# A fused cross-attention and sparse feed-forward kernel: norm factors through HBM instead of a second transposition

## What is computed

```python
q = layernorm(x)                       # over the 512 columns, b = 32, c = 64, n = 512
qh, kh, vh = Wq q, Wk ctx, Wv ctx      # 8 heads of 64
qh = softmax(qh, over the 64 of a head) * 64 ** -0.5
kh = softmax(kh, over n)
context = einsum('bhdn,bhen->bhde', kh, vh)
out = Wo @ einsum('bhde,bhdn->bhen', context, qh) + bo        # b, 64, 512
norm = maximum(sqrt(sum(out * out, over the 64 channels)), 1e-12)
x = x + out / norm * g * 8             # g: one gain per channel

y = layernorm(x)                       # feed-forward on 2048 rows of 512
inter = y @ c1.T @ c2.T                # rank 16, 1792 wide
idx = argmax of each block of 32 in inter                      # 56 per row
out = relu(w1[idx] @ y) @ w2t[idx]
return x + out
```

## Time and profile before

| | before |
|---|---|
| median of 3 runs | 764.79 us |
| the profiled execution | 764.77 us, span 762.7 us |
| granted TensorE clock | 0.991 of full (2.4 GHz) |
| TensorE busy | 739.2 us, 97% |
| DVE busy | 624.0 us, 82% |
| GpSimd busy | 486.9 us, 64% |
| ACT busy | 402.3 us, 53% |
| DMA | 66,376 packets, 55.23 MB, 40,704 of them under 512 B |

### The profile page before, as it was taken

The page is one execution under the profiler, slowest core; times in us unless marked ns, Lnnn a source line. Parts: engine busy times, 40 slices in busy tenths (PEclk is TensorE's granted clock), DMA queues, the critical chain, the costliest instruction groups (busy, mean ns, idle before and its releaser), DMA issues.

```text
span 762.7 us, 14646 instructions
## 1 busy us (share of the span) xinstructions
PE 739.2 (97%) x5210; PEld 565.2 (74%) x5210; DVE 624.0 (82%) x910; ACT 402.3 (53%) x773; POOL 486.9 (64%) x549
## 2 busy tenths in 40 slices
PE   8989999999999999999995999999999999999998
PEld 6555665665665666665664989989898998989896
DVE  7978999999999999999956778787777878777652
ACT  5879999999999999998831112102111110211010
POOL 3899999998888888677554363463536346363420
PEclk9999999999999999999997999999999999999999
DMA  6244334333333333221201203022130311211011
GB/s 166 63 113 118 104 102 130 97 105 104 98 81 97 94 83 97 70 72 56 76 18 26 78 20 105 21 52 76 24 102 21 104 21 49 78 22 49 20 53 34
DMA packets 66376, 55.23 MB, mean 72 GB/s; under 512 B 40704, under 2 KB 49536, under 8 KB 66304
## 3 DMA queue, kind: packets, MB, share of 16 engines
q1 hardware_dynamic: 65648, 53.57, 25.8%
q10 hardware_dynamic: 656, 0.72, 0.3%
HBM read 38.52 MB, written 8.39 MB: 62 GB/s over the span
## 4 chain that ended last, share of the span: by engine, by line
PE 71%; POOL 17%; DVE 4%; issue 3%; ACT 2%; SPq 2%; DMA 1%; DVEq 0%; POOLq 0%; ACTq 0%
PE slot L1113 20%; PE po L1131 10%; PE turn L1131 10%; PE po L1243 7%; POOL Q L534 7%; PE turn L1228 5%; PE slot L1269 4%; PE turn L1211 4%; PE slot L1283 3%; POOL weights_lo L483 3%; POOL c_low L516 2%; POOL x_low L473 2%; SPq L275 2%; PE slot L1095 2%; PE po L1254 1%
## 5 line engine op out<-in xcount | busy, mean ns | idle before, releaser
L534 POOL TENSOR_TENSOR Q<-Q,qrec 128x1024 f32<-128x1024 f32 x64 | 121.4, 1905 | 36.3 <-DVE qrec L775 36.3
L422 POOL TENSOR_TENSOR E<-E,rank 128x512 bf16<-128x512 bf16 (+1 forms) x64 | 71.1, 1111 | 108.6 <-DVE E L624 107.6
L1246 PE MATMUL po<-QT,G 128*64 128x512 f32 x256 | 116.9, 599 | 0.0
L1243 PE MATMUL po<-E,ctxT 128*64 128x512 f32 x256 | 116.9, 599 | 0.0
L945 ACT ACTIVATE E<-slot,neg_kmax 128x512 f32<-128x512 f32 x128 | 86.3, 686 | 8.8 <-DVE neg_kmax L761 8.5
L435 POOL TENSOR_TENSOR behind<-E,first 128x512 bf16<-128x512 bf16 (+1 forms) x64 | 60.4, 944 | 41.9 <-DVE first L632 41.7
L727 DVE TENSOR_REDUCE qmax<-slot 128x16 f32<-128x1024 f32 x64 | 75.3, 1217 | 12.6 <-PE slot L1283 12.6
L1243 PEld LDWEIGHTS po<-E,ctxT 128*64 128x64 f32 x256 | 32.3, 136 | 65.4 <-issue 58.5
L761 DVE TENSOR_REDUCE neg_kmax<-slot 128x2 f32<-128x1024 f32 x64 | 76.4, 1194 | 3.8 <-PE slot L1269 2.9
L767 DVE TENSOR_REDUCE qsum<-Q 128x16 f32<-128x1024 f32 x64 | 77.3, 1208 | 2.2 <-ACT Q L934 1.5
L953 ACT ACTIVATE E<-turn 128x512 f32<-128x512 f32 x128 | 74.8, 612 | 3.7 <-PE turn L1211 2.7
(11 more groups left out here) (185 smaller groups left out, 1970.0 us busy)
## 6 DMA issues: line engine op xcount, KB each, us to landing
c_in<-in_ctx SPq DMA_DIRECT2D x64, 128.0 KB, 2.6
x_in<-in_x SPq DMA_DIRECT2D x64, 128.0 KB, 2.6
stage<-in_ffn_w SPq DMA_DIRECT2D x32, 225.0 KB, 2.6
attn_out<-po_sb SPq DMA_DIRECT2D x32, 128.0 KB, 2.3
out<-E SPq DMA_DIRECT2D x16, 256.0 KB, 2.3
ctxT<-in_ctxT SPq DMA_DIRECT2D x31, 128.0 KB, 2.5
attn<-attn_out SPq DMA_DIRECT2D x9, 256.0 KB, 3.6
E<-attn_out SPq DMA_DIRECT2D x7, 256.0 KB, 4.0
```

Of the source, the lines that this page charges most:

```text
L534: nc.gpsimd.tensor_tensor(half, half, qrec[1 - par][:, s, :].unsqueeze(2).broadcast_to([P, HALF, D]), ALU.mult).then_inc(q_scaled, 1)
L1243: nc.tensor.matmul(po[0:C, :], ctxT[1 - par][:, m, :], E[1 - par][:, :, m * P:(m + 1) * P], start=(m == 0), stop=(m == NT - 1)).then_inc(p ...
L1246: nc.tensor.matmul(po[C:P, :], G[:, m, :], QT[m][:], start=(m == 0), stop=(m == HT - 1)).then_inc(out_mm, 1)
```

## The change

The transposed attention output is used for the norm alone. The squares stay in PSUM. The inverse norms, `[128 partitions, 8]` per tile (column n = 128 t + p, for batch b), are stored number by number into a new HBM buffer `factors` of shape `[16, 2, 512]`, and loaded back as a tile of `[128, 512]` in which the 512 numbers of a batch are repeated on its 64 channel partitions. DVE (for tiles 0 and 1 GpSimd) multiplies the attention output, which was never turned, by that tile. `turn_back`, `keep_turned` and `scale_kept` are gone.

```diff
-FIRST_ITEMS, PAIRS = 2, 12
+FIRST_ITEMS, PAIRS = 4, 14
+TURNS = (B - 8, B - 5)
+        over_channels = lambda a: factors[a].unsqueeze(1).broadcast_to([2, C, N])
+        by_token = lambda f: f.rearrange("b (t p) -> p (b t)", p=P)
+        inverted = lambda a: a + 1 if a < 2 else 2 + a // 2
...  SP, attention steps
+                def store_factor(a):
+                    sp.wait_ge(norm_inv, a + 1)
+                    sp.dma_start(by_token(factors[a]), inv[:, a], allow_slow_non_contiguous=True).then_inc(first_stored, 16)
+                def load_factor(a):
+                    sp.wait_ge(first_stored, 16 * (a + 1))
+                    sp.dma_start(spread_of(a), over_channels(a)).then_inc(spread_in[a], 16)
-                    if real(known, -2):
+                    if real(known, -2) and known < B + 1:
                         sp.wait_ge(po_copied, g)
                         sp.dma_start(scratch[g - 2], po_sb[par][C:P, :]).then_inc(stored[par], 16)
...  SP, duo
-                            sp.wait_ge(attn_turned, a - 1)
+                            sp.wait_ge(added, a - 1)
                             load_attn(a)
...  GpSimd
+                def scale(a):
+                    pool.wait_ge(spread_in[a], 16)
+                    nc.gpsimd.tensor_tensor(attn_of(a), attn_of(a), spread_of(a), ALU.mult).then_inc(scaled, 1)
                 def duo(d, last):
-                    rank_mask(d, 3)
-                    select(d, 2)
-                    rank_mask(d, 4)
                     select(d, 3)
                     if not last:
-                        invert(2 * d + 2)
+                        invert(2 * d + 2, 2)
                     rank_mask(d, 5)
                     select(d, 4)
-                    if not last:
-                        invert(2 * d + 3)
                     select(d, 5)
...  DVE
                 def scale(a):
-                    dve.wait_ge(norm_inv, a + 1)
-                    dve.wait_ge(attn_back, max(a - 1, 2))
-                    nc.vector.tensor_tensor(by_batch(turned_of(a)), by_batch(pre[t][:]), ...)
+                    dve.wait_ge(spread_in[a % 2], 16 * (a // 2 + 1))
+                    nc.vector.tensor_tensor(attn_of(a), attn_of(a), spread_of(a), ALU.mult).then_inc(scaled, 1)
                 def duo(d, last):
...
                     gate(d, 1)
-                    if not last:
-                        scale(a + 1)
                     block_max(d, 6)
                     h_low(d, 1)
-                    if not last:
-                        residual(a, pre[0])
                     gate(d, 2)
+                    if not last:
+                        for t in range(2):
+                            scale(a + t)
+                            residual(a + t)
+                            moments_of(a + t)
+                        normalize(a)
                     first_max(d, 6)
+                        normalize(a + 1)
                     block_max(d, 7)
...  ACT
+                def exchange(d):
+                    a = 2 * d + 2
+                    act.wait_ge(norm_inv, inverted(a))
+                    for t in range(2):
+                        nc.scalar.dma_start(by_token(factors[a + t]), inv[:, t], allow_slow_non_contiguous=True)\
+                            .then_inc(factors_stored, 16)
+                    act.wait_ge(factors_stored, 32 * (d + 1))
+                    act.wait_ge(scaled, a)
+                    for t in range(2):
+                        nc.scalar.dma_start(spread_of(a + t), over_channels(a + t)).then_inc(spread_in[t], 16)
                 def duo(d, last):
                     h_high(d, 0)
                     if not last:
-                        square(a, pre[0])
-                        square(a + 1, pre[1])
+                        exchange(d)
                     h_high(d, 1)
...  ACT, step
+                        if known == B + 1:
+                            act.wait_ge(po_copied, g)
+                            nc.scalar.dma_start(scratch[g - 2], po_sb[par][C:P, :]).then_inc(stored[par], 16)
...  TensorE, duo
-                    if not last_duo:
-                        turn_attn(a, pre[0])
-                        turn_attn(a + 1, pre[1])
...
-                        turn_back(a, pre[0])
-                        turn_back(a + 1, pre[1])
...
                     down(d, 3)
+                    if d + 2 < DUOS:
+                        turn_attn(a + 2, pre[0])
+                        turn_attn(a + 3, pre[1])
```

More of the change, by code:

```diff
@@ L78, in real, with program @@
     return known is None or 0 <= known + shift < B
-def program(nc, A, scratch, out):
+def program(nc, A, scratch, factors, out):
     with ExitStack() as ctx:
@@ L542, in step @@
                         bias(g + 2, par)
[L543 to L551, removed]
+                    if known in TURNS:
+                        invert(TURNS.index(known), 1)
+                    if known in (TURNS[0] + 1, TURNS[1] + 1):
+                        scale(TURNS.index(known - 1))
+                    if known in (B - 4, B - 2):
+                        prepare((known - (B - 4)) // 2)
+                        normalize((known - (B - 4)) // 2)
                     if known == B - 1:
@@ L671, in duo @@
                     gate(d, 1)
-                    if not last:
-                        scale(a + 1)
                     block_max(d, 6)
                     h_low(d, 1)
+                    gate(d, 2)
                     if not last:
-                        residual(a, pre[0])
-                    gate(d, 2)
+                        for t in range(2):
[3 more added lines that the diff above has]
+                        normalize(a)
                     first_max(d, 6)
                     if not last:
-                        residual(a + 1, pre[1])
-                    h_low(d, 2)
+                        normalize(a + 1)
                     block_max(d, 7)
[L684 to L687, removed]
                     if not last:
@@ L690, in duo @@
                         xT_rest(a + 1, pre[1])
+                    h_low(d, 2)
+                    first_max(d, 7)
                     gate(d, 3)
-                    h_low(d, 3)
                     gate(d, 4)
@@ L695, in duo @@
                         z_low(d + 1)
-                    h_low(d, 4)
+                    h_low(d, 3)
                     if not last:
@@ L1056, in turn_attn @@
                     last.then_inc(attn_turned, 1)
-                def turn_back(a, bank):
-                    pe.wait_ge(scaled, a + 1)
-                    if a < 2:
-                        pe.wait_ge(q_copied, HT * (B - 5 + a) + 4)
-                    for t in range(NT):
-                        last = nc.tensor.transpose(bank[:, t * P:(t + 1) * P], turned_of(a)[:, t * P:(t + 1) * P], ident[:])
-                    last.then_inc(attn_back, 1)
                 def turn_x(a, bank):
@@ L1145, in duo @@
                         down(d - 1, 6)
-                    else:
-                        project(d, 5)
                     project(d, 6)
                     hide(d, 2)
-                    if not last_duo:
-                        turn_back(a, pre[0])
-                        turn_back(a + 1, pre[1])
                     down(d, 0)
@@ L1292, in step @@
                         pe.wait_ge(rest_in, 32)
-                    if known in (B - 3, B - 2):
-                        turn_back(known - (B - 3), turn[(8 * g + 1) % 3])
+                    if known in TURNS:
+                        turn_attn(TURNS.index(known), turn[(8 * g) % 3])
+                    if known in (B - 2, B - 1):
+                        turn_x(known - (B - 2), turn[(8 * g) % 3])
                     for m in range(HT):
@@ L1314, in step @@
                     turn_e(3)
[L1315 to L1318 removed]
                     if known == B:
[L1320 removed]
                         project(0, 2)
                         project(0, 3)
+                        hide(0, 0)
+                        project(0, 4)
                     if known == B + 1:
[L1324 removed]
+                        turn_attn(2, pre[0])
+                        turn_attn(3, pre[1])
+                        project(0, 5)
                 steps(step)
```

191 lines of the change are left out of this document (94 added, 97 removed).

## The result

The changed kernel takes 911.5 us (median of four runs, 910.8 to 912.7) against 766.75 for the kernel before on the same chip: ratio 1.189 [1.184, 1.193], +145 us. The forecast was 822 us with a range of 747 to 850. The direction was right; the time is outside the range. The profiled execution took 910.75 us and has a span of 909.1.

A forecast was written before the change was run, and what follows sets the result against it. TensorE was taken as the bound, with 71% of the chain of waits and no slack in the duos. The terms 38 + 10 + 4.6 + 7.5 - 3 = +57 gave 822 us, its own range 780 to 860, all cases 747 to 850.

The forecast's parts named there:

- The chain's reading: Last 340 us, eight duos of 44.67 us: TensorE never waits, so any wait added ahead of a matmul is lost.
- The load: Repeating factor loads in a duo: confined to two DMA engines, landing 8.2 and 13.7 us after issue.
- Rival A: Whole kernel: repeating load confined by its outermost count of 2; duo 51 us, 822 us in all; chance 0.52.
- Rival B: Whole kernel: load spread over 16 engines, 4-byte writes at most 37 ns; 752 us (744 to 760); chance 0.33.
- Items: Attention loop: weight items start at step 4, two at a time for 14 steps; -3 us (-2 to -3.5).
- The wait of 3.4 us in step 3: Attention loop, step 3: TensorE's 3.42 us wait for GpSimd goes when its two pairs of items leave.
- The stores: Duo's 4-byte stores to HBM: 30 ns a packet, 3.8 us, plus 2.3 for a plain store and 0.5 issue.
- It adds nothing of its own: Duo: stores sharing engines with mask transposes, and SP's second half of masks behind load_attn, add no time of their own.
- ACT's blocked h_high(d,1): Duo: h_high stands behind ACT's wait for the stores; costed at nothing, with TensorE waiting at down(d,1) as its sign.
- the seam's delay of 4.6: Seam before the duos: with two engines the second load is in at 426.3, turn_x ends at 431.6, +4.6 us.
- 38 + 10 + 4.6: Us added: 38 over six duos, 10 for the slowed clock in seven duos, 4.6 at the seam.
- The attention end: End of attention loop: GpSimd's scale(0) and scale(1) wait for the round trip; -0.5, or +7.5 us (0 to +12).

The follow-up runs named there:

- the run with 32-byte rows: Changed kernel with inverse norms stored as 128 rows of 32 bytes instead of 1,024 single numbers per tile, loads unchanged, norms applied to wrong tokens: 816.2 us, ratio 1.067.
- both edits together: Changed kernel with inverse norms stored in 32-byte rows and repeating loads split to outermost count 64, norms applied to wrong tokens: 753.7 us, ratio 0.984.
- The run with stores alone: Changed kernel with its 4-byte stores, but only two rows of each factor tile loaded in the duos: 832.7 us, ratio 1.088.

## Why the prediction was wrong, step by step

**Right.** The chain's reading: a duo had no slack, and idle before turn_x went into the time. The load: two engines, 8.2 and 13.7 us forecast, 8.6 and 13.8 measured with cheap stores. By the Trainium skill ("DMA: Bandwidth & Descriptors", "Why a DMA increments its semaphore by 16 and not by 1") the outermost counts set the number of engines; here the load with an outermost count of 2 ran at a DMA share of 0.13, two of sixteen, and took 10.4 to 15.8 us, and with 64 it took 3.4 to 4.3, so the trace agrees. Rival A's duo of 51 us is the 51.3 of the run with 32-byte rows, and its 822 us that run's 816. Rival B's 752 is the 753.7 of both edits together. Items: -3 forecast, -3.1 measured. The wait of 3.4 us in step 3 is gone.

**The step that failed: "The stores".** I had each land 6.1 us after issue (2.3 + 3.8); in the duos it was 11.8. I took 30 ns per 4-byte piece on an engine, with 60 as the end. Between 128 and 16 pieces an engine (if spread over sixteen) the landing differs by 11.8 - 2.0 = 9.8 us, 88 ns a piece. Nor is the form of the term right, a price times the number of pieces: from 2.0 us for 16 pieces an engine, 88 ns would give a lone store of 1,024, 64 an engine, 6.2 us, and it took 11.4 and 9.9. The bound came from queue 1's mean packet, that is from the time that packets occupy in the records. That measure misses the cost: the 12,544 packets more than in the run with 32-byte rows add 2.3% x 16 x 909.1 - 1.8% x 16 x 812.0 = 101 us, 8 ns each, while in the duo above the landing comes 8 us after the last packet. An upper end from packets of 2 KB and 256 bytes was no bound for a write of 4.

**"It adds nothing of its own".** I named the mask transpositions that share engines with the stores and dismissed them. They are most of what the small writes cost in a duo. A transposition issued beside the stores lands with them; DVE is ready for gate(1) at 557.8 (564.99 - 7.21), in time for down(d,1), which TensorE reaches at 563.1 (567.65 - 4.51); it comes 7.2 us later and TensorE idles 4.5. The run with stores alone puts 8.3 us on a duo (51.8 for 43.5) with no wait at turn_x; the loads alone put 7.8 (51.3). Together they make 19.8 instead of 16.1. Most of the difference is at turn_x: per duo TensorE waits 6.6 us at down and 8.9 at turn_x (46.3 and 62.4 over seven), where the stores alone gave 7.0 at down and the loads alone 5.3 at turn_x. Late stores send the loads out late (564.73 - 553.14 = 11.6 us after the store, for 2.4 with 32-byte rows), and the stall at down, 6.6 us, covers only part of that. The forecast had a stall at down as a sign of ACT's blocked h_high(d,1). The stall came, and it was the mask.

**Sum.** From the two kernels' spans, 909.1 - 762.7 = 146.4: 15.5 up to duo 0's inverse (423.3 against 407.8), 113.3 in six duos (379.8 against 266.5), 17.6 behind. The last holds duo 6 with its own round trip. In the forecast the seam's delay of 4.6 is duo 0's turn_x, behind that inverse. So forecast were 53 behind it (38 + 10 + 4.6), measured 131, and 4.5 ahead of it (7.5 - 3), measured 15.5. The attention end went wrong by the same step: the lone stores of 1,024 pieces took 11.4 and 9.9 us where I had 4.2. With 32-byte rows and the same loads the inverse of duo 0 comes at 408.4, 15 us earlier. Rival A's 822 us therefore fits the run with 32-byte rows only because that run takes the stores' cost away: the division of the load was right, and the stores were not.

**Small errors.** The inverse ends 4.5 us after the duo's first down matmul (534.78 - 530.32 with both edits), not 2.3; the pow of sixteen takes 3.35 us, not 2.9. ACT's block, costed at nothing, shows no cost in the runs.

What stays open is why a transposition on SP's queue waits for the whole of ACT's small writes and is not served between them, and what makes 4-byte pieces land late when their packets are long over.

## What to carry to other kernels

Look at the size of a DMA's pieces, not at its bytes, and bound what they cost by landing times, not by the busy share of the queue or by the packets' own time. Fewer pieces of the same size, or more DMAs for them, did not help here; larger pieces did. A store of single numbers is paid by whoever has a transfer in flight beside it, so ask what that transfer releases before saying that the store is hidden. For a broadcast load, write the access so that the outermost count is large; for a column of numbers, one small transposition on TensorE before the store cost 0.1 us of TensorE and sent the store out 1.6 us later (5.0 us after the inverse starts, for 3.4), and it then landed in 1.4 us instead of 11.8.

## What was not expected of the hardware

Stores of the same 8 KB to HBM landed in 11.6 to 12.7 us in pieces of 4 bytes, in 4.9 with 8, in 3.1 with 16, in 2.0 with 32 and in 1.4 with 512. Half the 4-byte pieces still took 9.5 to 11.8 us. A DMA transposition on the other queue, 2.3 us otherwise, landed with them. In the window 560 to 562.7 above, when all packets of the 4-byte stores were over and they had not landed, the DMA share is 0.65 at 26 GB/s: some 100 ns for each 256-byte packet of the mask transpositions, an estimate from that row, where the prediction read 20 from the kernel before. A weight load with a stride of 16 bytes takes 210 ns for 141. "TensorE: Matmul & The Clock Gate" of the Trainium skill, section "LDWEIGHTS (loading the stationary operand)", counts columns alone; the strided row goes against that.
